# A two-layer attention, expert and feed-forward kernel: normalisations moved to VectorE, PSUM banks, SBUF homes and queues reassigned, and a new order of its steps

## What is computed

```python
x = x + _L0_xattn_ref(_layernorm(x), ctx, mask)      # attention 1
x = x + _L0_ffn_ref(_layernorm(x), Wr, Wg, Wu, Wd)   # experts
x = x + _L1_xattn_ref(_layernorm(x), W_qkv, W_o, ..., ctx, ctx, 54)   # attention 3
x = x + _L1_ffn_ref(_layernorm(x), w1, w2)           # quantised feed-forward

def _L0_ffn_ref(x, Wr, Wg, Wu, Wd):
    probs = softmax(x @ Wr)
    topk_w, topk_idx = top_k(probs, 2)
    topk_w = topk_w / sum(topk_w)
    for i in range(8):
        w_i = sum(topk_w * (topk_idx == i))
        output = output + w_i * ((silu(x @ Wg[i]) * (x @ Wu[i])) @ Wd[i])

def _L1_xattn_ref(x, W_qkv, W_o, ..., K_mem, V_mem, clip_k):
    scores = coef * einsum('bsd,bnd->bsn', (x @ W_qkv.T)[..., :D], K_mem)
    thr = top_k(scores, clip_k)[0][..., -1:]
    scores = where(scores < thr, -inf, scores)
    return (softmax(scores) @ V_mem) @ W_o.T
```

## Time and profile before

| | |
|---|---|
| median of 3 runs | 474.13 us (473.98 to 475.46) |
| profiled execution | 473.72 us, span 471.9 us |
| TensorE (PE) busy | 365.6 us, 77% |
| VectorE (DVE) busy | 295.2 us, 63% |
| ScalarE (ACT) busy | 174.6 us, 37% |
| GpSimd (POOL) busy | 81.0 us, 17% |
| mean granted clock of TensorE | 0.913 of full speed |
| moved by DMA | 76.38 MB, mean 162 GB/s |

### The profile page before, as it was taken

How to read it: one execution, slowest core, us unless ns; L and a number is a source line. 1 busy time by engine, 2 the same in 40 slices (tenths; PEclk the granted TensorE clock), 3 DMA queues, 4 the chain that set the end, 5 groups by cost and what they waited for, 6 DMA issues and landing times. The chain is left out here.

```text
span 471.9 us, 6596 instructions
## 1 busy us (share of the span) xinstructions
PE 365.6 (77%) x2078; PEld 287.3 (61%) x2082; DVE 295.2 (63%) x752; ACT 174.6 (37%) x295; POOL 81.0 (17%) x124
## 2 busy tenths in 40 slices
PE   0789999999998890796997998874999256815985
PEld 0457677777987880543586987763577145705773
DVE  3135453633211104349986899878497999998983
ACT  2153452433533310231345455622344333131574
POOL 5500140262000017372000000074010000000000
PEclk9999999999999997596998999997999869765998
DMA  8985345268299943089257776556152004320101
GB/s 260 375 275 172 95 151 158 86 211 285 65 287 328 291 141 134 11 279 368 78 154 237 238 248 218 189 162 219 33 169 90 11 11 140 93 97 7 50 2 56
DMA packets 70809, 76.38 MB, mean 162 GB/s; under 512 B 5356, under 2 KB 69496, under 8 KB 70776
## 3 DMA queue, kind: packets, MB, share of 16 engines
q1 hardware_dynamic: 65912, 67.80, 45.1%
q10 hardware_dynamic: 3328, 3.97, 2.5%
q0 software_dynamic: 1536, 4.20, 2.5%
HBM read 66.91 MB, written 9.04 MB: 161 GB/s over the span
## 5 line engine op out<-in xcount | busy, mean ns | idle before, releaser
L882 PE MATMUL GU<-xgT,ew_ring 128*128 128x128 f32 x480 | 59.9, 279 | 9.5 <-issue 5.4
L882 PEld LDWEIGHTS GU<-xgT,ew_ring 128*128 128x128 f32 x480 | 56.4, 193 | 14.6 <-issue 8.2
L611 ACT ACTIVATE pT<-T 128x512 f32<-128x512 f32 x64 | 31.8, 514 | 85.5 <-PE T L821 66.0
L821 PE MATMUL T<-ident,row 128*128 128x128 f32 (+1 forms) x208 | 34.1, 290 | 27.0 <-DVE row L1155 24.9
L1115 DVE MAX8 cand_h<-fold 128x8 f32<-128x801 f32 x56 | 54.2, 984 | 0.0
L839 PE MATMUL O<-pT,v_ring 128*128 128x128 f32 (+1 forms) x416 | 52.7, 285 | 1.9 <-ACT pT L611 1.7
L839 PEld LDWEIGHTS O<-pT,v_ring 128*128 128x128 f32 (+1 forms) x416 | 50.8, 200 | 4.2 <-issue 3.6
L807 PE MATMUL S<-k_ring,xT 128*128 128x400 f32 (+2 forms) x128 | 49.4, 523 | 3.1 <-ACT xT L596 3.1
L807 PE MATMUL S<-k_ring,qT 128*128 128x400 f32 (+2 forms) x128 | 48.7, 536 | 2.6 <-ACT qT L665 2.6
L835 PE MATMUL O<-v_ring,pT 128*128 128x256 f32 (+1 forms) x208 | 49.7, 381 | 0.0
L988 DVE CUSTOM_DVE_ANT_0 row<-S,mask_add 128x400 f32<-128x400 f32 (+2 forms) x32 | 18.4, 575 | 48.6 <-PE S L807 44.1
(11 more groups left out here) (153 smaller groups left out, 496.5 us busy)
## 6 DMA issues: line engine op xcount, KB each, us to landing
v_ring<-ctx SPq DMA_DIRECT2D x36, 512.0 KB
ew_ring<-Wg SPq DMA_DIRECT2D x30, 256.0 KB, 3.4
ew_ring<-Wu SPq DMA_DIRECT2D x30, 256.0 KB, 3.9
ew_ring<-Wd SPq DMA_DIRECT2D x30, 256.0 KB, 4.8
k_ring<-ctxT SPq DMA_DIRECT2D x16, 400.0 KB, 4.6
xg<-xs SPq DMA_DIRECT2D x30, 128.0 KB, 4.1
ys<-y_sb SPq DMA_DIRECT2D x30, 128.0 KB, 4.5
k_ring<-ctxT SPq DMA_DIRECT2D x8, 402.0 KB, 6.3
```

Source lines behind the costliest of these rows:

```text
L611: act.activation(pT[0:r, i % NPT, :, :].rearrange("p a s -> p (a s)")[:, 0:w], t_bank("pT", *key)[0:r, 0:w], ACT.Copy).then_inc(pTe_done, 1)
L821: mm = pe.transpose(t_bank(*step)[0:r, a * P:(a + 1) * P], src[:, m * P:m * P + r], ident[:, :])
L882: mm = pe.matmul(gu_bank(*key)[:, a * F + f * P:a * F + (f + 1) * P], ew_ring[:, w % NW, a, k, f * P:(f + 1) * P], xgT[:, i % NXGT, k, :], ...
```

## The change

- Layer norms: the two instructions of `norm` run on VectorE, no longer on GpSimd. `rstd` stays there. The steps take their rows from a table `ROWS` of pairs of tiles, the same pairs as the batches before.
- PSUM: value sums of both attentions have one bank of their own (`A`), every other sum has one bank (`O`). Before, all of them took turns on two.
- Keys: every chunk of each attention has its own home (2 x 4); a chunk is loaded again as soon as both tiles of the batch before have used it. Values: four groups for attention 1, and for attention 3 two homes in turn for the three large groups and one for the last.
- Weights of experts have three homes (four before), sorted rows three (four before). There is one mask home (two before), and four homes for transposed rows (two before).
- `xgl` and `yst`, the load and the store of sorted rows, are issued by ScalarE's queue, no longer by SyncE's.
- `DENSE = 0`: the new code for experts without sorting (`comb`) issues nothing.
- The whole `ORDER` is written anew. It loads and normalises batch 0 first, puts four tiles of experts of group 1 ahead of the first scores of attention 3, keeps a great part of the search of tile 3 for behind the experts of group 1, and puts much of block 4 of tiles 3 and 4 behind the last search. The two orders begin and go on like this:

```diff
-ldx.1 mask.0 ldx.0 ldx.2 ldk.1.0.2 ldx.3 ldk.1.0.0 ldk.1.0.1 ldk.1.0.3 zero fixed wload.1 mask.1 stats.1.1 stats.1.0
-aggr.1.0 var.1.0 stats.1.2 rstd.1.0 norm.1.0 aggr.1.2 var.1.2 stats.1.3 rstd.1.2 xT.1.0 aggr.1.3 norm.1.2 xTe.1.0
...
+ldx.0 mask.0 ldk.1.0.0 ldk.1.0.1 ldk.1.0.2 ldx.3 ldk.1.0.3 ldx.1 ldx.2 stats.1.0 aggr.1.0 var.1.0 rstd.1.0 norm.1.0
+xT.1.0 xTe.1.0 s1.0.0 stats.1.3 aggr.1.3 var.1.3 rstd.1.3 stats.1.1 s1.0.1 stats.1.2 ldv.1.0.0 aggr.1.2 var.1.2
...
-GROUPS = [(0, 1), (2, 3)]
+DENSE = 0
+ROWS = [(0, 1), (2, 3), (4, 5), (6, 7)]
+GROUPS = [(0, 1, 2, 3), (4, 5, 6, 7)]
-NK, NV, NW, NXG, NY, NYG = 5, 5, 4, 4, 3, 4
+NW, NXG, NY, NYG = 3, 3, 3, 4
...
-        k_ring = sb("k_ring", [P, NK, KC, 402])
-        v_ring = sb("v_ring", [P, NV, 4, D])
+        k_sb = sb("k_sb", [P, 2, NKC, KC, 402])
+        v_sb = sb("v_sb", [P, 22, D])
...
-        O_bank = [bank("O0"), bank("O1")]
+        O_bank = bank("O")
+        A_bank = bank("A")
...
                 elif op == "ldk":
-                    i = K_USE[step]
-                    if i >= NK:
-                        k_freed(sp, *K_BY[i - NK][1:])
+                    i = l // 2 * NKC + c
+                    if b:
+                        sp.wait_ge(s1_done if l == 1 else s3_done, max(n("s%d" % l, t, c) for t in (2 * b - 2, 2 * b - 1)))
...
-                elif op == "norm":
-                    l, b = key
-                    pool.wait_ge(rstd_done, n("rstd", l, b))
...
-                    for j in range(TB):
-                        last = pool.tensor_scalar(rows[:, j, :], x_res[:, 2 * b + j, :], mv[:, l - 1, b, j, 0:1],
-                                                  rstd[:, l - 1, b, j:j + 1], ALU.subtract, ALU.mult)
...
+                elif op == "norm":
+                    l, u = key
+                    dve.wait_ge(rstd_done, n("rstd", l, u))
...
+                        last = dve.tensor_scalar(x_row(l, t), x_res[:, t, :], mv[:, l - 1, t, 0:1], rstd[:, l - 1, t:t + 1],
+                                                 ALU.subtract, ALU.mult)
...
-                    sp.dma_start(xg[:, i % NXG, :], xs[j * P:(j + 1) * P, :]).then_inc(xg_in[i % NXG], 16)
+                    act.dma_start(xg[:, i % NXG, :], xs[j * P:(j + 1) * P, :]).then_inc(xg_in[i % NXG], 16)
...
-                    sp.dma_start(ys[g][j * P:(j + 1) * P, :], y_sb[:, i % NY, :]).then_inc(y_out[i % NY], 16)
+                    act.dma_start(ys[g][j * P:(j + 1) * P, :], y_sb[:, i % NY, :]).then_inc(y_out[i % NY], 16)
...
             def o_free(step):
                 i = O_USE[step]
-                if i < 2:
+                if i < 1:
                     return
-                op, *key = O_BY[i - 2]
+                op, *key = O_BY[i - 1]
...
+            def a_free(l, t):
+                i = A_USE[(l, t)]
+                if i < 1:
+                    return
+                before_l, before_t = A_BY[i - 1]
+                if before_l == 1:
+                    pe.wait_ge(x1_done, n("x1", before_t))
+                else:
+                    pe.wait_ge(aTe_done, n("aTe", before_t))
```

631 lines of the change are left out of this document (339 added, 292 removed).

## The result

The changed kernel takes 452.29 us (median of 4 runs, 448.47 to 452.68) against 474.06 for the kernel before on the same chip: ratio 0.952 (95% interval 0.946 to 0.957). The profiled execution took 452.51 us, its span 450.8.

The account below looks back on a forecast made before the run. The prediction took TensorE to bound the early part and VectorE the end: first fold, VectorE's work from there, and its waits. Terms 7.3 - 0.7 - 0.4 - 10.9 + 2.6 = -2.1 took 473.7 to 471.6 us, range 459 to 486.

Parts of the forecast that it names:

- The start: Up to group 0's first expert: 4.5 us gained at the first scores, cancelled by 4.5 us of TensorE idling; 0.
- Experts of group 0: Group 0's expert stage: added work 9.1 us, less 3.8 of idle time filled, plus 2 for weights; +7.3, bounds +3 and +13.
- My 2 us for the third home: Group 0's last two experts: weight reloads of 6.0 us fit badly with three homes instead of four; 2 us.
- To the first fold: Group 0's last expert to second attention's first folded row: 35.3 us for 36.0, so -0.7, bounds -8 and +6.
- VectorE's work: From the first fold on: two normalisations add 1.2 us, four experts' products already done take off 1.7; -0.4.
- the pairs: Within VectorE's waits: 24 instructions now directly follow the one whose result they need; 1.6 us, bounds 1 and 7.
- VectorE's waits: VectorE's idle time from first fold to last search: 17.5 us against 28.4; -10.9, bounds -18 and 0.
- (a): First fold to 307: VectorE's idle time, much of it for late experts' products, falls from 12.9 to 8 us.
- (b): Round the second gathers: VectorE's 10.6 us of idle time falls to 3, covered by kept search work of tile 3.
- The tail: Behind the last search: more work stands there, 9 us of idle time for 6.4; +2.6, bounds 0 and +8.
- Filled without cost: Rival on experts: SyncE's queue paced them, so added work fits in (+3) and VectorE waits 12; 461.8 us, chance 0.15.
- Three homes too few: Rival on experts: weight reloads outlast the work over them, group 0 takes 4.5 us more, products late; 485 us, chance 0.31.

Follow-up runs that it names:

- e9: The changed kernel with a fourth home for experts' weights, room taken from attention 3's values, same order: 452.47 us, 0.964 of the kernel before.
- e7: The changed kernel with all experts of group 1 moved back, the first four behind the first scores of attention 3: 494.50 us, 1.043 of the kernel before.
- e10: The changed kernel with 20 VectorE steps moved by one to three places, so fewer instructions directly follow the one they need: 450.11 us, 0.960 of the kernel before.
- e16: The same kernel as e10, measured again on another chip beside the change: 450.89 us, 0.955 of the kernel before.
- e8: The changed kernel with 14 search steps of tile 3 (13 us) moved from behind group 1's gathers to ahead of the last expert's product: 469.29 us, 0.986 of before.
- e1: The kernel before with the change's new order, 29 of 1383 steps placed later to avoid blocking: 479.15 us, 1.020 of the kernel before.
- e6: The changed kernel with value sums and all other sums taking turns on two shared banks, 26 steps later: 480.16 us, 1.014 of the kernel before.
- e3: The changed kernel with loads and stores of sorted rows issued by SyncE again, same order: 455.57 us, 0.967 of the kernel before.
- e11: The kernel before with three weight homes instead of four, weight loads later where they would block: 519.70 us, 1.103 of the kernel before.
- e2: The changed code with the old order, 118 of 1383 steps placed later, mostly loads: 535.05 us, 1.136 of the kernel before.
- e13: The changed code with a fourth weight home and the old order, 92 steps placed later: 488.24 us, 1.037 of the kernel before.

## Why the prediction was wrong

**The view of the bound** was right: three numbers, first fold, VectorE's work, VectorE's waits. The side of faster was right too, though at a chance of 0.46 and with the most likely case at 467 to 477 it was no more than a lean; 2.5 us were forecast where 21.8 are measured.

**The start.** First scores forecast at 11.4, measured 11.52. The ranks came at 93.1 instead of 96, TensorE idled 3.43 us before the first sorted rows for 4.5. So 3 us of the gain were left at the first expert, where I had 0 (2.9, 2.8 and 4.7 in the three profiles).

**Experts of group 0.** +7.3 forecast, +13.1 measured (61.2 for 48.1; 11.7 and 15.2 in the other two profiles). The work that came in is what I had, 8.9 us (54.23 for 45.33) for 9.1. What failed is the term of -3.8 for idle time to be filled: TensorE idles 7.7 of 61.9 us, more and not less. My 2 us for the third home stood on the right mechanism; the waits for weights there are 4.3 us, 3.1 of them at the last two experts, and a fourth home makes the stage 2.9 to 6.4 us shorter (e9), so 2 was too small.

**To the first fold.** -0.7 forecast, -6.7 measured (-3.5 and -6.4 in the other two). The failed step here is "four experts of group 1 now stand ahead of the scores on TensorE, 4 x 2.9 us": they stand in a wait, and cost at most some tenths of a us (e7). I added their time to the path although showed 11.71 us of waiting there, and left the clock at its lower level, though with work in the gap it stays higher (0.76 to 0.88 for e7's 0.62).

**VectorE's work.** -0.4, and 1.6 for the pairs under the waits; measured +3.7 (231.45 for 227.78 with 488 instructions in both). The lengths of the 488 instructions sum to the same, 258.6 and 258.8 us; what grew is that 50 more of them start only when the one ahead has ended, 21 ahead of the last search and 29 behind it. e10 and e16 give their price, 0.07 to 0.08 us of busy time each. I had counted only 24, all ahead of the last search, and priced those in the waits.

**VectorE's waits: the failed step that decided.** I took 17.5 us to be left of 28.4, and 1.9 are; that is 15.6 of the 19 us by which the forecast missed. Each part was right in its direction and cut short. (a) 8 of 12.9 for late products: 0.6 is left (75.5 - 74.88). I argued from the number of products, eleven for fifteen. What counts is who leads: TensorE starts group 1 four experts ahead and has 67.11 us of work for VectorE's 74.88 in that stretch, so no product is late. (b) 3 round the gathers: 0.9, and e8 shows the kept search to be worth 10 of them. (c) "The rest stays 4.9" had no ground; it is 0.4. Of the 1.9 us left, 0.9 are the 27 gaps of some 0.03 us between dependent instructions. What I missed is that a queue which is always behind its suppliers has no waits at all, and waits do not shrink in proportion. That this lead is the cause in (a) is argued from the busy times; e1 has it too, and e7, which takes it away, has 21.1 us of waits there, but e7 moved more than the four experts.

**The tail.** +2.6 of idle time forecast, -1.3 measured (5.1 for 6.4). The moved work covers the chain of the last tile; the last three outputs wait for TensorE for 3.5 us in sum. The single bank costs little: e1 and e6, with two, have tails of 31.5 and 31.7 for 32.0.

**The rivals.** "Filled without cost" was nearest (461.8), for a wrong reason: nothing was filled for free in the experts. For it I had read the pace of 3.34 us as that of SyncE's queue; the stage itself ran at 3.27 us an expert (49.1 / 15), and by e3 the queue brings at most 1.6% of the total. The 0.85 us an expert for this has no working; two issues of 0.39 are 0.78. "Three homes too few", at 0.31, did not make the kernel slower, but half of its condition is there: the waits for weights sum to 8.1 us, over the 6 that I had named as a sign of being wrong. The sign was badly placed, since 3.8 of them fall where VectorE is behind. In the old order the third home costs 50 us, nearly four times the 13 I gave it (e11). I had read the reload's cover for the new order, and priced it for the last two experts only. The Trainium skill ("Trainium Kernel Development and Optimization", Best Practices) advises to double-buffer, which three homes do as well as four, so it did not speak against the third home as I had it. The runs say how far more homes help: e2 to e13 pays 47 us for the third to the fourth home where the order has no slack, e9 nothing in the total where it has.

## What to carry to other kernels

Order, banks and homes are one design: the order without the new code made the kernel slower (1.020), and so did the new code without its order (1.136, with a fourth home 1.037); together they take 4 to 5% off. For an engine that bounds a stretch, ask for every wait in its queue whether its supplier leads when that place is reached; if all lead, the waits go to zero, and only work counts. Count the distance from a buffer's release to its next use for every use in the order, and compare it with one measured reload.
